# A two-layer transformer block on one core: one software pipeline over the batches, score tiles on 24 rows, shared weighing tiles and spreads by DMA

## What is computed

```python
x = x + attn1(layernorm(x))             # retention: no softmax
x = x + block2(layernorm(x))

def attn1(x):                           # layer one, "retained"
    q, k = rope(x @ Wq.T), rope(x @ Wk.T); v = x @ Wv.T
    qk = (q @ k.T) / sqrt(8) * decay    # causal, decay gamma_h ** (n - m)
    out = groupnorm_per_head(qk @ v) * gn_weight + gn_bias
    return out @ Wo.T

def block2(x):                          # layer two
    h = rms(x) * n1_w
    q, k, v = rms_heads(h @ wq.T), rms_heads(h @ wk.T), h @ wv.T
    a = softmax(causal(q @ k.T * 8**-0.5)) @ v
    x = x + [a @ wo.T, first 32 channels set to 0]
    xf = rms(x) * n2_w
    w = top2(softmax(xf @ gate_w.T))    # of 4 experts, all of which are computed
    return x + [sum_e w[e] * expert_e(xf), first 32 channels set to 0]
```

## Time and profile before

| | us |
|---|---|
| time, median of 3 runs (1051.55 to 1053.09) | 1051.71 |
| profiled execution, its own time | 1052.72 |
| its span, first to last instruction | 1050.9 |
| TensorE matmuls busy | 866.0 |
| VectorE busy | 682.8 |
| ScalarE busy | 507.0 |
| GpSimd busy | 171.4 |
| mean granted TensorE clock | 0.899 of 2.4 GHz |

### The profile page before, as it was taken

How to read it: one execution, slowest core, us unless ns; L and a number is a source line. 1 busy time by engine, 2 the same in 40 slices (tenths; PEclk the granted TensorE clock), 3 DMA queues, 4 the chain that set the end, 5 groups by cost and what they waited for, 6 DMA issues and landing times.

```text
span 1050.9 us, 15987 instructions
## 1 busy us (share of the span) xinstructions
PE 866.0 (82%) x4513; PEld 500.2 (48%) x4560; DVE 682.8 (65%) x1825; ACT 507.0 (48%) x1080; POOL 171.4 (16%) x218
## 2 busy tenths in 40 slices
PE   2646897898878897898987897898977989879967
PEld 1524454464435554364543654455543645436434
DVE  6467936788368854789368873688457883578431
ACT  1313473456544474455644465454644556444634
POOL 5310202022010301013020210104020220202002
PEclk9575898899989998899988999799988989889979
DMA  4101210030100301021100301003100201003000
GB/s 142 40 11 24 47 33 20 1 71 13 41 11 0 81 5 46 0 50 31 40 11 0 81 1 40 11 10 71 29 22 0 59 22 40 1 0 81 2 0 11
DMA packets 27893, 31.57 MB, mean 30 GB/s; under 512 B 5184, under 2 KB 16064, under 8 KB 27840
## 3 DMA queue, kind: packets, MB, share of 16 engines
q1 hardware_dynamic: 23616, 28.92, 11.9%
q10 hardware_dynamic: 4224, 2.10, 0.7%
HBM read 5.58 MB, written 2.10 MB: 7 GB/s over the span
## 4 chain that ended last, share of the span: by engine, by line
PE 67%; DVE 20%; issue 6%; ACT 4%; DMA 1%; SPq 0%; DVEq 0%; POOL 0%; ACTq 0%; POOLq 0%
PE ring L593 9%; PE outs L560 8%; PE side L629 8%; DVE mxp L1058 6%; PE side L666 6%; PE ring L580 5%; PE ring L449 4%; PE ring L441 3%; PE side L644 3%; PE outs L460 3%; PE side L441 3%; PE single L435 2%; PE ring L596 2%; PE single L509 2%; PE ring L540 2%
## 5 line engine op out<-in xcount | busy, mean ns | idle before, releaser
L1058 DVE TENSOR_REDUCE mxp<-ring 128x4 f32<-128x512 f32 x320 | 204.8, 684 | 31.6 <-PE ring L580 25.6
L789 ACT ACTIVATE p<-ring 128x512 f32<-128x512 f32 x320 | 173.6, 603 | 67.5 <-PE ring L596 43.6
L593 PE MATMUL ring<-qx,ks 128*128 128x512 f32 x320 | 141.8, 497 | 20.7 <-DVE mxp L1058 19.2
L580 PE MATMUL ring<-kx,qs 128*128 128x512 f32 x320 | 147.3, 509 | 2.5 <-DVE mxp L1058 0.4
L1159 POOL TENSOR_SCALAR_AFFINE_SELECT p<-p 128x512 f32<-128x512 f32 x64 | 39.7, 635 | 311.9 <-ACT p L698 310.8
L593 PEld LDWEIGHTS ring<-qx,ks 128*128 128x128 f32 x320 | 62.4, 201 | 59.2 <-DVE mxp L1058 27.7
L560 PE MATMUL outs<-p,v 128*32 128x512 f32 (+3 forms) x1024 | 87.7, 442 | 0.7
L580 PEld LDWEIGHTS ring<-kx,qs 128*128 128x128 f32 x320 | 63.5, 202 | 37.2 <-DVE mxp L1058 23.8
L1053 DVE COPY oT<-outs 128x512 f32<-128x512 f32 x32 | 22.0, 689 | 89.7 <-PE outs L560 89.7
L435 PE MATMUL single<-sb_t_id,nat 128*128 128x128 f32 x128 | 27.2, 351 | 59.3 <-DVE nat L1086 29.6
L666 PE MATMUL side<-sb_w_dn,h 128*128 128x96 f32 x384 | 51.9, 276 | 6.0 <-ACT h L817 6.0
(11 more groups left out here) (169 smaller groups left out, 1602.2 us busy)
## 6 DMA issues: line engine op xcount, KB each, us to landing
qx<-qs SPq DMA_DIRECT2D x32, 256.0 KB, 4.6
qx<-qs SPq DMA_DIRECT2D x32, 192.0 KB, 3.6
kx<-ks SPq DMA_DIRECT2D x96, 64.0 KB, 2.0
x_in<-x_dram ACTq DMA_DIRECT2D x8, 256.0 KB, 3.0
qx<-qs SPq DMA_DIRECT2D x32, 64.0 KB, 2.0
qx<-h SPq DMA_DIRECT2D x128, 2.0 KB
out_dram<-yout SPq DMA_DIRECT2D x8, 256.0 KB, 2.3
sb_t_cos<-t_cos_dram SPq DMA_DIRECT2D x1, 512.0 KB, 5.5
```

The costliest lines, as they stand in the source:

```text
L580: last = nc.tensor.matmul(dst[:, :], qs[:, g, qt * 128:(qt + 1) * 128], kx[:, g % 2, :, kt * 128:(kt + 1) * 128], start=True, stop=kt < qt)
L593: last = nc.tensor.matmul(dst[:, :], ks[:, g, kt * 128:(kt + 1) * 128], qx[:, g, :, qt * 128:(qt + 1) * 128], start=True, stop=kt < qt)
L789: A_(p2(kt)[:, :, (qt - kt) * 128:(qt - kt + 1) * 128], pr[(U_AB + at) % 4][:, :].rearrange("p (j n) -> p j n", j=J), ACT.Exp, scale=float ...
L1058: V.tensor_reduce(mxp[:, qt, :, kt], ring(b, U_AB + at)[:].rearrange("p (j n) -> p j n", j=J), AX.X, ALU.max).then_inc(max_read, 1)
```

## The change

All stages now lie in one Python loop over 12 iterations `it` from -2 to 9, without a device loop. An iteration has eight places (`NF`) and then 32 steps (`G * GK`). In the places stand the experts of batch `it-2` and the retained scores and weighing of batch `it+1`. Step `s` has, on each engine, an exponential unit (two heads, one key tile) 16 steps behind, the maximum unit `s` of batch `it`, and the stages `before` (batch `it+1`), `tail` (`it-1`), `lead` (`it+2`), `down` (`it-2`), weighing and the transposes of the maxima where the tables name a step. The old code is replaced nearly everywhere; what follows are the new tables and functions that carry the work, with the old ones that they replace.

```diff
-AHEAD = 14
-ORDER = MAXIMA[:NU + AHEAD] + mixed(EXPS, MAXIMA[NU + AHEAD:]) + EXPS[(G - 1) * NU - AHEAD:]
-LEAD_AT = (9, 14, 19, 24, 29, 34, 39, 44, 49, 54, 59, 64, 69)
-FFN_AT = {"start": (0,), "scored": (1,), "weighed": (2,), "spread": (3,), "projected": (4, 5), "normed": (6, 7)}
+GK = NT * NH
+LAG = 2 * GK
+FIRST, LAST = -2, B + 2
+WEIGH_AT = {5: (-1, 2, 0), 9: (-1, 2, 1), 13: (-1, 3, 0), 17: (-1, 3, 1), 21: (0, 0, 0), 25: (0, 0, 1), 29: (0, 1, 0)}
+MT_AT = {1: (-1, 3), 9: (0, 0), 17: (0, 1), 25: (0, 2)}
-        pr = [pb(f"ring{i}", [128, 512]) for i in range(4)]
-        ps = pb("single", [128, 512])
-        px = [pb(f"side{i}", [128, 512]) for i in range(2)]
+        mb = pb("maxima", [128, 2, 512])
+        eb = pb("scores", [128, 2, 512])
+        px = [pb(f"side{i}", [128, 512]) for i in range(3)]
...
 # TensorE, maxima of two heads: 24 rows each, then the mask in four pieces of 32 rows
-                        last = nc.tensor.matmul(dst[:, :], qs[:, g, qt * 128:(qt + 1) * 128],
-                                                kx[:, g % 2, :, kt * 128:(kt + 1) * 128], start=True, stop=kt < qt)
+                if count(max_read, b, k) > 0:
+                    pe.wait_ge(max_read, count(max_read, b, k))
+                for i in range(2):
+                    rows = slice(SW * (2 * hp + i), SW * (2 * hp + i) + SHIFT)
+                    nc.tensor.matmul(mb[:, i, 0:n + 128], qs[rows, b % 2, g, n:n + 128], ks[rows, b % 2, g, 0:n + 128],
+                                     start=True, stop=False, skip_group_check=True)
+                for r in range(J):
+                    for i in range(2):
+                        rows = slice(SW * (2 * hp + i), SW * (2 * hp + i) + SW)
+                        last = nc.tensor.matmul(mb[:, i, n + SW * r:n + 128], idq[rows, r, :], ngq[rows, r, SW * r:128],
+                                                start=False, stop=r == J - 1, skip_group_check=True)
...
 # TensorE, scores for the exponentials: 25 rows, no mask (POOL cuts them after the exponential)
+                if count(exp_done, b, i8) > 0:
+                    pe.wait_ge(exp_done, count(exp_done, b, i8))
+                for i in range(2):
+                    rows = slice(SW * (2 * hp + i), SW * (2 * hp + i) + SHIFT + 1)
+                    last = nc.tensor.matmul(eb[:, i, 0:n], ks[rows, b % 2, g, 128 * kt:128 * kt + 128],
+                                            qs[rows, b % 2, g, 128 * kt:T], start=True, stop=True)
...
 # TensorE, retained scores of one row tile: 16 matmuls on 24 rows
+                for j in range(J):
+                    dst = side(f"SC{t}{j}", b)
+                    rows = slice(SW * j, SW * j + SHIFT)
+                    for g in range(G):
+                        last = nc.tensor.matmul(dst[:, 128 * g:128 * g + 128], ks1[rows, g, at], qs1[rows, g, at],
+                                                start=True, stop=True)
...
 # TensorE, weighing: two groups of heads share one bank, 16 rows each
+                        at = SW * (J * g + j) + (2 * D, 0)[a]
+                        last = nc.tensor.matmul(po[SW * j:SW * j + SW, 128 * kt:T], v2x[:, b % 3, kt, at:at + SW],
+                                                p2[kt][:, j, :], start=a == 0 and kt == 0, stop=a == 1 and kt == NT - 1,
...
 # VectorE
-                        V.tensor_reduce(mxp[:, qt, :, kt], ring(b, U_AB + at)[:].rearrange("p (j n) -> p j n", j=J),
-                                        AX.X, ALU.max).then_inc(max_read, 1)
+                dve.wait_ge(m_filled, count(m_filled, b, k + 1))
+                V.tensor_reduce(mneg[:, g, 2 * hp:2 * hp + 2, qt], mb[:, :, 0:128 * (qt + 1)], AX.X, ALU.max, negate=True)\
+                    .then_inc(max_read, 1)
...
 # SyncE: the high and low parts go to their rows by DMA, 24 for a layer; stack and its matmuls are gone
+            def spread(dst, parts, order, signal):
+                for j in range(J):
+                    for r, part in enumerate(order):
+                        sp.dma_start(dst[SW * j + D * r:SW * j + D * r + D, :, :].bitcast(f32),
+                                     parts[SW * j:SW * j + SW, part, :]).then_inc(signal, 16)
...
 # before(b), step 19
+                    spread(qs[:, b % 2], qhl, (0, 0, 1), spread2_q)
...
+                    spread(ks[:, b % 2], khl, (0, 1, 0), spread2_k)
 # lead(b), step 26
+                    spread(qs1, qhl, (0, 0, 1), spread1_q)
...
+                    spread(ks1, khl, (0, 1, 0), spread1_k)
```

More of the change, by code:

```diff
@@ L13 @@
 SHIFT = 3 * D
+PERM = np.array([D * (J * g + j) + d for j in range(J) for d in range(D) for g in range(G)])
 M0 = 32
@@ L73, in tables @@
+FILLED = []
+for it in range(FIRST, LAST):
+    for place in sorted(SIDE_UNITS):
+        FILLED += [(name, it + off) for off, name in SIDE_UNITS[place] if 0 <= it + off < B]
+UNIT = {u: i for i, u in enumerate(FILLED)}
 def tables():
@@ new lines, in retain @@
+                if t:
+                    nc.tensor.matmul(po[:, at], state[:, t - 1, :], qT[:, at], start=True, stop=False, skip_group_check=True)
+                for j in range(J):
+                    for g in range(G):
+                        w = SHIFT + SW * (J * g + j) - D * j
+                        last = nc.tensor.matmul(po[SW * g:SW * g + SW, at], v1x[:, t, w:w + SW],
+                                                p1[:, t % 2, j, 128 * g:128 * g + 128], start=t == 0 and j == 0, stop=j == J - 1,
+                                                skip_group_check=True)
@@ new lines, in up, with experts @@
+            def up(name, b, w, m, src, blocks=1):
+                dst = side(name, b)
+                n = w.shape[-1] // blocks
+                for k in range(blocks):
+                    last = nc.tensor.matmul(dst[:, :], w[:, k * n + m * 128:k * n + (m + 1) * 128], src(k),
+                                            start=k == 0, stop=k == blocks - 1)
+                last.then_inc(side_filled, 1)
+            def experts(b, place):
+                whole = lambda k: xfT[:, :]
+                if place in (0, 1):
+                    up(f"G{place}", b, ww["w_g1"], place, whole)
+                    up(f"U{place}", b, ww["w_u1"], place, whole)
+                if place == 2:
+                    for m in range(2):
+                        up(f"L1{m}", b, ww["w_l1"], m, whole)
+                    up("D3", b, ww["w_d3"], 0, whole)
+                if place == 3:
@@ L900, in lead @@
[L900 to L909 removed]
+                    i = V.bn_aggr(mv[:, n, t, :], stats[:, n, t, :])
@@ L1226, in _ @@
-            Q.memset(qx[:].bitcast(f32), 0.0).then_inc(consts_ready, 1)
-            Q.memset(kx[:].bitcast(f32), 0.0).then_inc(consts_ready, 1)
-            pool.wait_ge(rotation_loaded, 16 * len(ROTATION))
-            pool.wait_ge(stack_cleared, 1)
-            run(pool, lead, front, attend, lambda b, part: None, down, lambda: None)
+                    Q.tensor_tensor(qk, qk, sq, ALU.add).then_inc(qk1_ready, 1)
+                if s == 26:
+                    pool.wait_ge(qT_ready, count(qT_ready, b, 1))
+                    pool.wait_ge(high1_ready, count(high1_ready, b, 1))
+                    Q.tensor_tensor(qhl[:, 1, :].bitcast(f32r), qT[:, :], qhl[:, 0, :], ALU.subtract).then_inc(low1_q, 1)
@@ L1296, in _ @@
+            load(0)
             for name in PROJECTION:
```

1775 lines of the change are left out of this document (823 added, 952 removed).

## The result

The changed kernel takes 1355.2 us (1353.9 to 1360.3), the kernel before 1051.7: a ratio of 1.289, 95% interval 1.286 to 1.293. Slower, as forecast, but by 304 us and not 148, and above the range. The profiled execution took 1353.9 us for a span of 1352.0.

What follows compares the result with a forecast made beforehand. TensorE and its waits were taken as the bound; full iterations of 92 (steps) + 36 (experts' part) + 6 (standing), plus the ends, summed to 1198 us of span, with 1.8 around it 1200 us; range 1020 to 1300.

Steps and rivals of the forecast that it cites:

- The cadence is TensorE's, and only 16 us of it can be won: Kernel before: 120.7 us a batch, mostly TensorE matmuls; a schedule leaving that work as is gains at most 16 us.
- Places, 36: Eight places opening an iteration: experts' matmuls, retained scores and weighing take 36 us, between 32 and 40.
- Spread, 24 x 0.59 + 2.0 = 16 us, of which 6 stand: Retained layer's 24 DMAs take 16 us; steps 27 to 31 cover about 10, so TensorE stands about 6 an iteration.
- rival D: Spread much later, only if a DMA issue costs 1.63 us: 39 us a spread, 1320 us in all; chance 0.02.
- A turn, 0.9 us: Steps: hand-over from VectorE's reduction through TensorE's `maxima` fill and back costs 0.9 us, between 0.65 and 1.35.
- rival A: Faster: TensorE runs ahead, row tiles cost their lower bound, half the turns stay; 980 us, chance 0.22.
- A change of tile shape, 0.3 us: TensorE: each switch between tile shapes costs about 0.3 us, in 22 of 32 steps and twelve times in the experts' part.
- Steps 92 at full clock: The 32 steps of an iteration take 92 us, 87 with lower prices and 102 with upper; TensorE alone has 67.
- turns which neither engine can fill decide: Steps: with one pair of banks for `maxima`, some 25 us a batch are turns neither TensorE nor VectorE can fill.
- Ends: Filling and emptying iterations: 40, 86, 108 and 108 us up to iteration 1; 130, 90, 68 and 32 for the last four.
- Rival C: Slower by the clock: steps run a third of the time at the lower level, adding 90 us, 1290 in all; chance 0.11.
- my likeliest case: The forecast itself: 1200 us, 14% slower, with chance 0.50 for 1060 to 1270.

Runs made afterwards that it cites:

- slack two: Kernel before, with TensorE in the mixed part of attention filling a ring bank only when the unit two places earlier was read, not four: 1194.4 us.
- the short reductions: Changed kernel, with VectorE's reductions of the maxima reading only the first 128 columns of each head: 1293.1 us.

## Why the prediction was wrong

The sign and its reasons held; the size didn't. Point by point, with the sum's own terms:

- *The cadence is TensorE's, and only 16 us of it can be won.* Right: the new schedule made the work no smaller, 109.5 us busy in the iteration shown, and added waits of 35.
- *Places, 36.* Right: 35.2.
- *Spread, 24 x 0.59 + 2.0 = 16 us, of which 6 stand.* **This step failed.** It is 26 us: issues at 0.70, landing 8.7 behind. I took the landing from the earlier trace rows, DMAs of the same bytes but to 32 partitions; the run with 32 partitions has 16.6 us and a stand of 5.5 to 7.2. That the last steps cover 10 us was right. The eight stands were 26, 25.7 and six of 13.6 to 16.3, 142 us together; the sum had 17, 17 and six of 6 (one of them inside the 130 of iteration 6): 70. With the wait in step 25 (the run without it is 26 us faster; the sum had 7) the slow landing makes 72 + 19, about 90 of the 154 us by which span and sum differ; the two runs that take it away one part at a time give 57 and 26. My rival D had an issue at 1.63 us as the only way for it to be late, and the landing in none. Its price was summed wrong, too: 39 us of issue in place of 14 are 25 more a spread and not 15, so that D stood near 1400 and not at 1320.
- *A turn, 0.9 us.* Too dear for full clock, where it is 0.6 in the mean; right for the lower level, at which it is 0.9 and which the sum didn't assume. The mask matmuls start 0.03 us apart, the side of rival A. By eights of steps iteration 3 has 26, 28, 22.5 and 19 us, the sum had 28, 25, 20 and 19.
- *A change of tile shape, 0.3 us.* Too dear: at full clock a matmul of another shape starts 0.10 to 0.11 us behind the last mask, and the scores on 25 rows 0.20 us behind a matmul of 128 rows, where another of 128 rows starts after 0.11. The sum had 6.6 + 3.6 us of such changes in an iteration; no run takes them away.
- *Steps 92 at full clock.* 99: cheaper turns against a clock of 0.70 to 0.75, at which TensorE was busy 79 us and not 67, and 4 us of ScalarE's wait. Errors of both signs met here, so the near hit is no proof of the sum.
- *That turns which neither engine can fill decide.* Right: 17.8 us a batch from slack two in the kernel before, and up to 8.5 of 12.8 us in the short reductions.
- *Ends.* Up to the end of the steps of iteration 1 the sum had 342 us, the trace has 405.7; the last four had 320, the trace 349. Besides the stands the clock goes with it: in iterations -1 to 1 it is 0.50 to 0.70, and the retained part took 21.3, 19.6 and 22.3 us for 16. I had put prices of a full clock on stretches in which TensorE mostly waits. No run held the clock up there, so its part in what the ends lost beside the stands is argued, not shown.
- *Rival C, a clock under 0.85.* It came true, in the steps and the ends, beside my likeliest case and not in its place. I had made cases that add up exclude each other; my case with C's 90 us is 1290, and with the landing's 90 us on top 1380, where 1355 was measured.

## What to carry to other kernels

Price a DMA by how many partitions it writes as much as by its bytes (8 and 32 were tried here), and look for a row of the same shape before taking a landing time. A wait for one pair of banks costs each unit its fill and both hand-overs, and lowers the clock at which the fill runs; keep several units of slack between engines, even if tiles get larger for it. When the likeliest case and a rival can both be true, add them before drawing the range.

## What the runs showed of the hardware

- DMAs of 64 KB to 8 partitions each: 60 to 68 GB/s, a landing 8.7 us behind the last of 24 issues; to 32 partitions, 103 GB/s and 1.5 us.
- Two engines' queues issuing DMAs to 8 partitions each: 28 us for a spread, one queue 26.
- A fill of `maxima` and its hand-over, 512 columns: 0.65 to 0.70 us at full clock, 1.13 at the lower level.
- The same work of the places takes 33.8 us at a granted clock of 0.90 and 37.7 at 0.81.
- Two heads' fills on 24 and 32 rows with 128 columns: 0.31 us side by side, 0.49 one after the other, at full clock.
- Behind the last mask (32 rows), a matmul with another tile shape starts 0.10 to 0.11 us later at full clock.
- TensorE busy 78 to 81% of the steps, with clocks of 0.70 to 0.75: a high busy share went with a low clock, and at the lower clock the same matmuls take longer and fill more of the time.
